# Reordering the turn from the second head pair to the mixture of experts: statistics, drains, norm, filler matmuls, one weight split

## The chip, the cores and the metric

The kernel runs on one core of one Trainium2 chip. The metric is the device time of one launch in microseconds. The time before is 760.16 us, the median of 3 runs (759.25 to 761.29).

## What is computed

One launch runs two transformer layers on 1024 rows of 256 columns, in fp32 accuracy. Each layer is modulated by a vector c: `mod = silu(c) @ wmod` gives shift, scale and gate for its two halves.

- Layer 0: `x += ga * attention(LN(x)*(1+ca)+sa)` (16 heads of 128, 4 key/value heads, rotary, causal), then `x += gb * ffn(LN(x)*(1+cb)+sb)` with a 2:4-sparsified gated unit.
- Layer 1: `x += ga * (h + attention(rmsnorm(h)))` with 4 heads of 64 over 2 key/value heads, not causal, where h is the modulated layer norm; then `x += gb * moe(LN(x)*(1+cb)+sb)`.
- The mixture has one shared expert and 7 routed ones, each `(x1 * silu(x2)) @ w2` with 256 columns in, 2 x 128 inside. A sigmoid of the gate's logits picks two experts per row, and each expert keeps the 146 rows of its highest scores (ties by row order). The kept rows' outputs are weighted by their score and added.

The change touches the end of layer 1's attention and the mixture.

## The kernel before, in words

Each engine has its own program, written out in order; semaphores tie them together. PE is the matmul engine, ACT, DVE and POOL do elementwise work, SP starts transfers. Every fp32 operand of a matmul is kept as a high and a low half, and a product is three matmuls (`product`, L56 to L60): high*high and the two of a high with a low half. Nearly always ACT writes the high half out of PSUM (`..._hi`), and DVE or POOL subtracts it to get the low one (`..._lo`). `keep_warm` (L63) issues filler matmuls into a PSUM area that nobody reads. The kernel is three blocks, with a barrier of all engines between them.

**The end of the attention (`ffn0_attention1`).** The loop over s handles 32 tiles of scores (4 heads x 8 row tiles; HS = 32), with the stages of one tile 3 steps apart (LAG): scores, maximum on DVE, exponential on ACT, scaling on POOL, eight 128x128 transposes on PE (`turn`), high half (`probs_hi`, ACT) and low half (`probs_lo`, DVE). Four tiles make a chunk, whose values product (`attend`, four parts of four matmuls) comes 7 steps behind, so the last chunk (7) is attended in s = 35 to 38, after the last `turn(31)` in s = 34. Its sum is drained by `attended_hi(7)` on ACT and `attended_lo(7)` on DVE. The second head pair's output product is four jobs `out_job(1, j)` of 12 matmuls, each for two row tiles; 0 and 1 need only the chunks of the first row half and run at s = 31 and 32, 2 and 3 need chunk 7 (L1365). DVE adds each to x (`add_out`).
The next layer norm starts here: DVE takes statistics of row tiles 0 to 3 (`final_stats`, at s = 33), aggregates them (`variances`), POOL takes the inverse root (`inverse_roots`), DVE makes a bias of it (`spread`), ACT normalizes four tiles (L1537), PE transposes them (L1361 to L1364), ACT scales and shifts (`ln_h32`), DVE splits the result into `hT` (L1745 to L1749). PE ends the block with 10 fillers (L1367).

**The mixture (`ffn1`).** PE's order: the logits of the first row half (`find_logits(0)`), `up(0)`, `up(1)`, transposes of the second row half (`turn_x`), `up(2)`, `find_logits(1)`, `up(3)`, `turn_logits`, `up(4)`, and then `up(n)` and `count(n - 5)` in turn. `up(n)` is the first product of one expert for one row half, 12 matmuls of 512 columns. The slots are

```
slots = [(0, 0), (1, 0), (2, 0), (0, 1), (1, 1), (2, 1)] + [(e, c) for e in range(3, E8) for c in range(2)]
```

so slot 6 is the first of expert 3. `up(n)` waits for its expert's split weights (`w1_ready`, a count in order of the experts: `split_hi` on ACT, `split_lo` on DVE for 0 and 1, on POOL for the others) and for `mid_done` of slot n - 2, which frees its PSUM banks. Behind each `up`, ACT does `activate`, DVE `middle`, ACT `feed_hi`, POOL `feed_lo`. In the kernel before, POOL splits expert 3 behind `feed_lo(4)`, and ACT's high half of it stands behind `activate(4)`.
The second row half's statistics (tiles 4 to 7) are taken by DVE at the start of this block; its normalized, transposed and scaled rows are split by DVE in `split_x` (L2106), behind `middle(1)`, and `find_logits(1)` waits for that.
Routing: DVE marks the best two (`mark_best`), then ten rounds of `compare` (DVE), `count` (PE) and `raise_cut` (DVE) find each expert's cut; `find_order` (PE) and `weigh` (DVE) settle ties and give `row_weight`. The PSUM areas that `weigh` reads lie in the banks p_y[2] and p_y[3]. Then `down(e)`, the second products, two row tiles at a time (j = 0 to 3, into p_y[j]); the first of them waits for `weight_done`.

Of the kernel before, what the change touches and what calls it, by code (L numbers as in the profile page):

```python
# [16 lines left out]
S = 1024  # L17
# [961 lines left out]
def ffn0_attention1(nc, a, m, sems, sb, split):  # L979
# [6 lines left out]
    with ExitStack() as ctx:  # L986
# [130 lines left out]
        with nc.Block() as block:  # L1117
# [30 lines left out]
            def _(pe):  # L1148
# [195 lines left out]
                for s in range(HS + ATT):  # L1344
                    if s < HS:
                        scores(s)
                    chunk, part = divmod(s - ATT, 4)
                    if s >= ATT and part:
                        attend(chunk, part)
                    if LAG <= s < HS + LAG:  # L1350
                        turn(s - LAG)
                    if s >= ATT and not part:
                        attend(chunk, part)
                    for n, _ in jobs_of(s):
                        if n >= len(first):
                            project(n)
                    for pair_index, j in out_slots.get(s, ()):
                        out_job(pair_index, j)
                pe.wait_ge(turn_lo, 2 * HS)
                pe.wait_ge(ln_normed, len(FIRST_TILES))  # L1360
# [4 lines left out]
                for j in range(2, 4):  # L1365
                    out_job(1, j)
                keep_warm(pe, p_scores[1][:, BANK:S], m.room, 10)  # L1367

            @block.scalar
            def _(act):  # L1370
# [167 lines left out]
                for n in FIRST_TILES:  # L1538
                    act.activation(ln_xn[:, n, :], m.x[:, n, :], ACT.Identity, scale=m.rstd[:, n:n + 1], bias=m.nbias[:, n:n + 1]).then_inc(ln_normed, 1)
                attended_hi(2 * H1 - 1)  # L1540
# [6 lines left out]
            def _(dve):  # L1547
# [175 lines left out]
                for s in range(HS + LAG):  # L1723
# [4 lines left out]
                    if 1 <= s <= HS:  # L1728
                        inverse_sum(s - 1)
                    if s > ATT and (s - ATT) % 4 == 3:  # L1730
                        attended_lo((s - ATT) // 4)
# [7 lines left out]
                    if s == HS + 1:  # L1739
                        final_stats(FIRST_TILES)  # L1740
                        variances(dve, m, chain, FIRST_TILES)
                dve.wait_ge(m.sqrt_out, FFN_ROOTS + CHUNKS + 2)
                spread(dve, m, FIRST_TILES).then_inc(spread_ready, 1)
                attended_lo(2 * H1 - 1)
                for k in range(KD):  # L1745
                    cols = slice(0, BANK)
                    dve.wait_ge(ln_scaled, k + 1)
                    chain.run(dve.tensor_copy(m.hT.hi[:, k, cols], ln_h32[:, k, :]))
                    dve.tensor_tensor(m.hT.lo[:, k, cols], ln_h32[:, k, :], as_f32(m.hT.hi[:, k, cols]), ALU.subtract)  # L1749
                add_out(1, 2)  # L1750
# [98 lines left out]
def ffn1(nc, a, m, sems, sb, split):  # L1849
# [4 lines left out]
    with ExitStack() as ctx:  # L1854
# [63 lines left out]
        with nc.Block() as block:  # L1918
# [15 lines left out]
            def _(pe):  # L1934
# [52 lines left out]
                def down(e):  # L1987
                    pe.wait_ge(w2_ready, e + 1)
                    pe.wait_ge(fed_lo, max(n for n, s in enumerate(slots) if s[0] == e) + 1)
                    if e == 0:  # L1990
                        pe.wait_ge(weight_done, 1)
                    for j in range(PAIRS):
                        if e == 1:
# [33 lines left out]
            def _(act):  # L2027
# [29 lines left out]
                load_table(act, m, ACT.Sigmoid, 2)  # L2057
                activate(0)
                act.wait_ge(spread_ready, 1)
                for n, t in enumerate(LAST_TILES):  # L2060
                    act.activation(xn[:, n, :], m.x[:, t, :], ACT.Identity, scale=m.rstd[:, t:t + 1], bias=m.nbias[:, t:t + 1]).then_inc(normed, 1)  # L2061
                feed_hi(0)
                activate(1)
# [4 lines left out]
                read_logits(0)  # L2068
                feed_hi(1)
                activate(2)  # L2070
                read_logits(1)
                feed_hi(2)
# [7 lines left out]
                for n in range(4, len(slots)):  # L2080
                    e, c = slots[n]
                    activate(n)
                    if c == 1 and 3 <= e + 2 < E8:
# [6 lines left out]
            def _(dve):  # L2090
# [72 lines left out]
                split_lo(1)  # L2163
                for n in LAST_TILES:
                    chain.step(dve.bn_stats(m.stats[:, n, :], m.x[:, n, :]))  # L2165
                variances(dve, m, chain, LAST_TILES)
                dve.memset(aff[:], -1.0).then_inc(aff_cleared, 1)
# [41 lines left out]
            def _(pool):  # L2209
# [19 lines left out]
                pool.wait_ge(m.staged, 48 + 160)  # L2229
                split_lo(2)  # L2230
                inverse_roots(pool, m, LAST_TILES, 11)
                for n in range(len(slots)):
                    e, c = slots[n]
                    feed_lo(n)
                    if c == 1 and 3 <= e + 2 < E8:
# [77 lines left out]
```

## Time and profile before

| | |
|---|---|
| median of 3 runs | 760.16 us |
| profiled execution, own time | 754.2 us |
| its span, first to last instruction | 752.4 us |
| PE busy | 701.7 us (93% of the span), 4301 matmuls |
| DVE / ACT / POOL busy | 551.8 / 441.4 / 386.3 us |
| mean granted PE clock | 0.997 |
| bytes moved | 19.85 MB, mean 26 GB/s |

All is one profiled execution. Times in the rows are us from the start of its span. A busy PE is not a PE at its peak, since matmuls overlap and their ends are modelled: what counts is the time from one start to the next. The number in square brackets behind a row is idle time of that engine just before it, and the instruction that ended it. Granted clock 1.00 is 2.4 GHz.

### The profile page before, as it was taken

The page shows a single profiled execution, that of the slowest core. Times are in us where ns is not written, and L with a number is a line of the kernel's source. Part 1 is how long each engine was busy: PE and PEld are TensorE (multiplying, and loading weights), DVE is VectorE, ACT ScalarE, POOL GpSimd, SP SyncE. Part 2 cuts the span into 40 slices and gives each one's busy share as a digit, 9 for nine tenths or more (in the row PEclk, how much of TensorE's full clock was granted, in tenths as well). Part 3 has the DMA queues.
Part 4 walks back from the last instruction along what each step waited for, and adds up shares of the span by engine and source line. Part 5 has one row for each costly group of instructions (what it writes and reads, how often), then busy time and mean ns, then how long its engine had stood idle before and what let it go on. Part 6 is the DMA issues. An engine that isn't in the chain of part 4 may idle for free. (4 is left out here: it accounts for less than half of the span.)

```text
span 752.4 us, 12234 instructions
## 1 busy us (share of the span) xinstructions
PE 701.7 (93%) x4301; PEld 604.0 (80%) x4301; DVE 551.8 (73%) x1234; ACT 441.4 (59%) x921; POOL 386.3 (51%) x421
## 2 busy tenths in 40 slices
PE   7979989999999999999998889999989999788997
PEld 5858878888888888888887779998767787666787
DVE  4567686768776877677776868989788788564666
ACT  3756656667566666666575545234588777544432
POOL 3876556645864477533662322312498344124773
PEclk9999999999999999999999999999999999999999
DMA  7000001000000000005001023000100000000001
GB/s 258 15 8 8 8 22 57 8 8 15 22 9 15 8 15 8 14 8 182 8 16 42 1 77 94 1 1 5 52 2 1 1 2 1 1 2 1 1 1 58
DMA packets 19131, 19.85 MB, mean 26 GB/s; under 512 B 2174, under 2 KB 17022, under 8 KB 19070
## 3 DMA queue, kind: packets, MB, share of 16 engines
q1 hardware_dynamic: 17950, 18.40, 7.6%
q8 instruction: 35, 0.57, 0.3%
q10 hardware_dynamic: 1120, 0.66, 0.3%
q14 instruction: 26, 0.21, 0.1%
HBM read 18.01 MB, written 1.05 MB: 25 GB/s over the span
## 5 line engine op out<-in xcount | busy, mean ns | idle before, releaser
L909 POOL TENSOR_TENSOR at_swapped<-at_swapped,at_sin 128x512 f32<-128x512 f32 x40 | 52.1, 1303 | 129.3 <-ACT at_swapped L588 129.3
L610 ACT ACTIVATE at_probs<-at_probs,at_negmax 128x128 f32<-128x128 f32 (+7 forms) x128 | 99.6, 778 | 31.8 <-DVE at_negmax L710 29.9
L710 DVE CUSTOM_DVE_ANT_0 at_probs<-at_scores,causal 128x128 f32<-128x128 f32 (+7 forms) x128 | 96.1, 750 | 17.4 <-PE at_scores L60 16.3
L501 PE MATMUL at_turn<-ident_sb,at_probs 128*128 128x128 f32 x576 | 85.0, 274 | 11.2 <-DVE at_full_T_lo L726 9.1
L501 PEld LDWEIGHTS at_turn<-ident_sb,at_probs 128*128 128x128 f32 x576 | 66.5, 140 | 19.8 <-issue 11.4
L603 ACT ACTIVATE at_edge_T_hi<-at_turn 128x128 fp32r<-128x128 f32 (+3 forms) x128 | 55.5, 434 | 33.4 <-PE at_turn L501 33.0
L58 PE MATMUL at_scores<-at_kT_hi,room 128*128 128x512 f32 (+1 forms) x192 | 66.3, 345 | 3.4 <-DVE at_negmax L710 3.4
L603 ACT ACTIVATE at_full_T_hi<-at_turn 128x512 fp32r<-128x512 f32 x64 | 38.2, 597 | 49.8 <-PE at_turn L501 47.6
L59 PE MATMUL at_scores<-at_kT_lo,room 128*128 128x512 f32 (+1 forms) x192 | 66.6, 347 | 0.0
L60 PE MATMUL at_scores<-at_kT_hi,room 128*128 128x512 f32 (+1 forms) x192 | 66.4, 346 | 0.0
L726 DVE TENSOR_TENSOR at_edge_T_lo<-at_turn,at_edge_T_hi 128x128 fp32r<-128x128 f32 (+3 forms) x128 | 61.3, 479 | 1.3 <-ACT at_edge_T_hi L603 0.8
L913 POOL TENSOR_TENSOR at_plain<-at_plain,at_swapped 128x512 f32<-128x512 f32 x40 | 51.8, 1296 | 6.1 <-POOL at_swapped L909 0.5
L740 DVE SCALAR_TENSOR_TENSOR x<-at_proj,at_rinv,x 128x256 f32<-128x256 f32 x122 | 52.8, 474 | 0.1
L731 DVE TENSOR_TENSOR at_att_lo<-at_att,at_att_hi 128x512 fp32r<-128x512 f32 x32 | 22.1, 692 | 38.4 <-ACT at_att_hi L617 38.4
L726 DVE TENSOR_TENSOR at_full_T_lo<-at_turn,at_full_T_hi 128x512 fp32r<-128x512 f32 x64 | 44.1, 689 | 7.1 <-ACT at_full_T_hi L603 5.4
L58 PEld LDWEIGHTS at_scores<-at_kT_hi,room 128*128 128x128 f32 x192 | 36.2, 188 | 9.5 <-issue 2.6
L918 POOL TENSOR_TENSOR room<-at_plain,room 128x512 fp32r<-128x512 f32 x32 | 41.4, 1292 | 2.7
L700 DVE TENSOR_TENSOR at_plain<-at_scores,at_cos 128x512 f32<-128x512 f32 x30 | 20.8, 692 | 29.9 <-ACT at_swapped L588 29.9
L58 PE MATMUL at_att<-at_edge_T_hi,at_v 128*128 128x512 f32 (+3 forms) x128 | 42.0, 328 | 0.0
L60 PE MATMUL at_att<-at_edge_T_hi,at_v 128*128 128x512 f32 (+3 forms) x128 | 41.3, 323 | 0.0
L58 PE MATMUL at_proj<-at_wo_hi,at_att_hi 128*128 128x256 f32 x122 | 39.5, 324 | 1.9 <-DVE x L740 1.8
L59 PE MATMUL at_att<-at_edge_T_lo,at_v 128*128 128x512 f32 (+3 forms) x128 | 41.1, 321 | 0.0
(446 smaller groups left out, 2257.7 us busy)
## 6 DMA issues: line engine op xcount, KB each, us to landing
at_wq_in<-L_attn_Wqkv SPq DMA_DIRECT2D x16, 128.0 KB, 2.2
at_wo_in<-L_attn_Wo SPq DMA_DIRECT2D x16, 128.0 KB, 2.0
staging<-L_ffn_routed_w SPq DMA_DIRECT2D x7, 256.0 KB, 4.3
wmod<-L_wmod SPq DMA_DIRECT2D x2, 768.0 KB, 4.3
at_wmod<-L_wmod SPq DMA_DIRECT2D x1, 1024.0 KB, 9.3
staging<-L_ffn_w_gate SPq DMA_DIRECT2D x1, 1024.0 KB, 5.3
staging<-L_ffn_w_up SPq DMA_DIRECT2D x1, 1024.0 KB, 7.4
staging<-L_ffn_w_down SPq DMA_DIRECT2D x1, 1024.0 KB, 9.8
```

The lines of the kernel that those rows point to most:

```text
L58: pe.matmul(out, left.hi, right.hi, start=start, stop=False)
L59: pe.matmul(out, left.hi, right.lo, start=False, stop=False)
L60: return pe.matmul(out, left.lo, right.hi, start=False, stop=stop)
L501: mm = pe.transpose(p_turn[t % 2][:, b - b0, :], probs[:, s % 4, b * P:(b + 1) * P], m.ident[:, :])
L603: act.activation(turned_columns(c, b0, b1, i % 4).hi, p_turn[t % 2][:, 0:b1 - b0, :], ACT.Copy)\
L610: act.activation(row, row, ACT.Exp, scale=-1.0, bias=negmax[:, unit % 4:unit % 4 + 1], accum_out=rowsum[:, unit // NT % 2, i:i + 1])\
L710: dve.tensor_tensor_reduce(out=probs[:, s % 4, 0:width], in0=p_scores[s % 2][:, 0:width], in1=m.causal[:, S - width:], scale=-1.0, scalar= ...
L726: dve.tensor_tensor(out.lo, p_turn[t % 2][:, 0:b1 - b0, :], as_f32(out.hi), ALU.subtract).then_inc(turn_lo, 1)
L740: ins = dve.scalar_tensor_tensor(out=rows, in0=bank[:, t * DM:(t + 1) * DM], scalar=rinv[:, head % 2, 2 * j + t:2 * j + t + 1], in1=rows, ...
L909: turning = pool.tensor_tensor(swapped[:, r % 2, :], swapped[:, r % 2, :], sin[:, cols], ALU.mult)
L913: chain.step(pool.tensor_tensor(turned, turned, swapped[:, r % 2, :], ALU.add))
L918: pool.tensor_tensor(out.lo[:, cols], turned, as_f32(out.hi[:, cols]), ALU.subtract).then_inc(rope_done, 1)
```

## The change

It moves the statistics of the first row half to two places (tiles 0 and 1 at s = 33, tiles 2 and 3 with the aggregation at s = 34, behind `attended_lo(6)` and `probs_lo(31)`), takes the drain of chunk 7 between the second and third normalized tile on ACT, puts `out_job(1, 2)` ahead of the norm's transposes and `add_out(1, 2)` ahead of the splits on DVE, takes the statistics of tiles 4 and 5 already in this block, and has 5, 6 and 8 fillers in three places in the place of 10 at the end. In the mixture, DVE takes statistics of tiles 6 and 7 alone and ahead of expert 1's low half, POOL takes the roots ahead of expert 2's low half, ACT changes the order of `activate(1)`, `feed_hi(0)` and `read_logits(0)` and drops one `load_table`, expert 3 is split behind `read_logits(1)` (ACT) and `feed_lo(2)` (POOL), and `down(0)` waits for `weight_done` at j = 2.

```diff
--- before.py
+++ after.py
@@ -1356,15 +1356,18 @@
                             project(n)
                     for pair_index, j in out_slots.get(s, ()):
                         out_job(pair_index, j)
+                    if s == HS + LAG - 1:
+                        keep_warm(pe, p_scores[1][:, BANK:S], m.room, 5)
                 pe.wait_ge(turn_lo, 2 * HS)
+                keep_warm(pe, p_scores[1][:, BANK:S], m.room, 6)
+                out_job(1, 2)
                 pe.wait_ge(ln_normed, len(FIRST_TILES))
                 for k in range(KD):
                     for n in FIRST_TILES:
                         mm = pe.transpose(turn_banks[k][:, n * P:(n + 1) * P], ln_xn[:, n, k * P:(k + 1) * P], m.ident[:, :])
                     mm.then_inc(ln_turned, 1)
-                for j in range(2, 4):
-                    out_job(1, j)
-                keep_warm(pe, p_scores[1][:, BANK:S], m.room, 10)
+                out_job(1, 3)
+                keep_warm(pe, p_scores[1][:, BANK:S], m.room, 8)
 
             @block.scalar
             def _(act):
@@ -1536,8 +1539,9 @@
                             job_high(n)
                 act.wait_ge(spread_ready, 1)
                 for n in FIRST_TILES:
+                    if n == 2:
+                        attended_hi(2 * H1 - 1)
                     act.activation(ln_xn[:, n, :], m.x[:, n, :], ACT.Identity, scale=m.rstd[:, n:n + 1], bias=m.nbias[:, n:n + 1]).then_inc(ln_normed, 1)
-                attended_hi(2 * H1 - 1)
                 for k in range(KD):
                     act.wait_ge(ln_turned, k + 1)
                     act.activation(ln_h32[:, k, :], turn_banks[k], ACT.Identity, scale=m.modcol[:, 1, 8 + k:9 + k], bias=m.modcol[:, 1, 6 + k:7 + k])\
@@ -1727,6 +1731,8 @@
                         job_low(len(first) - 1)
                     if 1 <= s <= HS:
                         inverse_sum(s - 1)
+                    if s == HS + 1:
+                        final_stats(range(0, 2))
                     if s > ATT and (s - ATT) % 4 == 3:
                         attended_lo((s - ATT) // 4)
                     if s >= LAG:
@@ -1736,18 +1742,19 @@
                             job_low(n)
                     for pair_index, j in out_slots.get(s, ()):
                         add_out(pair_index, j)
-                    if s == HS + 1:
-                        final_stats(FIRST_TILES)
+                    if s == HS + 2:
+                        final_stats(range(2, 4))
                         variances(dve, m, chain, FIRST_TILES)
                 dve.wait_ge(m.sqrt_out, FFN_ROOTS + CHUNKS + 2)
                 spread(dve, m, FIRST_TILES).then_inc(spread_ready, 1)
                 attended_lo(2 * H1 - 1)
+                add_out(1, 2)
+                final_stats(range(4, 6))
                 for k in range(KD):
                     cols = slice(0, BANK)
                     dve.wait_ge(ln_scaled, k + 1)
                     chain.run(dve.tensor_copy(m.hT.hi[:, k, cols], ln_h32[:, k, :]))
                     dve.tensor_tensor(m.hT.lo[:, k, cols], ln_h32[:, k, :], as_f32(m.hT.hi[:, k, cols]), ALU.subtract)
-                add_out(1, 2)
                 add_out(1, 3)
 
             @block.gpsimd
@@ -1987,9 +1994,9 @@
                 def down(e):
                     pe.wait_ge(w2_ready, e + 1)
                     pe.wait_ge(fed_lo, max(n for n, s in enumerate(slots) if s[0] == e) + 1)
-                    if e == 0:
-                        pe.wait_ge(weight_done, 1)
                     for j in range(PAIRS):
+                        if e == 0 and j == 2:
+                            pe.wait_ge(weight_done, 1)
                         if e == 1:
                             pe.wait_ge(shared_added, j + 1)
                         elif e:
@@ -2054,21 +2061,21 @@
                 split_hi(0)
                 split_hi(1)
                 split_hi(2)
-                load_table(act, m, ACT.Sigmoid, 2)
+                read_logits(0)
                 activate(0)
                 act.wait_ge(spread_ready, 1)
                 for n, t in enumerate(LAST_TILES):
                     act.activation(xn[:, n, :], m.x[:, t, :], ACT.Identity, scale=m.rstd[:, t:t + 1], bias=m.nbias[:, t:t + 1]).then_inc(normed, 1)
+                activate(1)
                 feed_hi(0)
-                activate(1)
                 for k in range(KD):
                     act.wait_ge(turned, k + 1)
                     act.activation(h32[:, k, :], p_turn[k], ACT.Identity, scale=m.modcol[:, 1, 8 + k:9 + k], bias=m.modcol[:, 1, 6 + k:7 + k])\
                         .then_inc(scaled_h, 1)
-                read_logits(0)
                 feed_hi(1)
                 activate(2)
                 read_logits(1)
+                split_hi(3)
                 feed_hi(2)
                 activate(3)
                 act.wait_ge(aff_cleared, 1)
@@ -2080,7 +2087,7 @@
                 for n in range(4, len(slots)):
                     e, c = slots[n]
                     activate(n)
-                    if c == 1 and 3 <= e + 2 < E8:
+                    if c == 1 and 4 <= e + 2 < E8:
                         split_hi(e + 2)
                     feed_hi(n)
                 for e in range(1, E8):
@@ -2160,10 +2167,10 @@
                     dve.tensor_tensor(row_weight[:, :, :], score[:, :, :], kept[:, :, :], ALU.mult).then_inc(weight_done, 1)
 
                 split_lo(0)
-                split_lo(1)
-                for n in LAST_TILES:
+                for n in range(6, 8):
                     chain.step(dve.bn_stats(m.stats[:, n, :], m.x[:, n, :]))
                 variances(dve, m, chain, LAST_TILES)
+                split_lo(1)
                 dve.memset(aff[:], -1.0).then_inc(aff_cleared, 1)
                 chain.step(dve.memset(best2[:], -1.0))
                 dve.memset(ones[:], 1.0)
@@ -2227,12 +2234,14 @@
 
                 chain = m.pool_chain.on(pool)
                 pool.wait_ge(m.staged, 48 + 160)
+                inverse_roots(pool, m, LAST_TILES, 11)
                 split_lo(2)
-                inverse_roots(pool, m, LAST_TILES, 11)
                 for n in range(len(slots)):
                     e, c = slots[n]
                     feed_lo(n)
-                    if c == 1 and 3 <= e + 2 < E8:
+                    if n == 2:
+                        split_lo(3)
+                    elif c == 1 and 4 <= e + 2 < E8:
                         split_lo(e + 2)
                     elif n >= 6:
                         split_w2(n // 2 - 3 if n < 13 else n - 9)
```

## Rows read from the trace of the kernel before

**Rows 1.** PE's timeline, end of attention: start, length, line, tile, idle before.

```profile
647.10 1.16 PE L1277 MATMUL l_turn<-ident_sb,staging 128*128 128x128 f32 x8
651.32 0.50 PE L1291 MATMUL l_att_sum<-l_pT_hi,l_v 128*128 128x512 f32 x1 [3.06 <-DVE l_pT_lo L1651]
...
655.14 1.04 PE L1363 MATMUL l_turn<-ident_sb,l_probs 128*128 128x128 f32 x8
656.92 0.36 PE L58 MATMUL l_scores<-l_wo_hi,l_att_hi 128*128 128x256 f32 x1 [0.74 <-DVE l_att_lo L1656]
...
659.86 2.44 PE L67 MATMUL l_scores<-room 128*128 128x512 f32 x10
662.60 0.39 PE L58 MATMUL ff_y<-hT_hi,gate_w_hi 128*7 128x512 f32 x1 [0.30 <-PEq L1117]
```

**Rows 2.** Who waited for whom, 640 to 726 us: total us, times, longest us.

```profile
PE ff_y L58 <- DVE hT_lo L2111: 1.6, 1, 1.6
...
PE ff_y L58 <- DVE ff_row_weight L2160: 0.9, 1, 0.9
```

**Rows 3.** PE's timeline in the mixture, around up(6).

```profile
686.04 0.41 PE L1972 MATMUL ff_y<-ff_above,ff_ones 128*128 128x64 bf16 x8
689.75 0.50 PE L58 MATMUL ff_px<-hT_hi,room 128*128 128x512 f32 x1 [3.31 <-POOL ff_w_lo L2214]
...
694.43 0.48 PE L58 MATMUL ff_px<-hT_hi,room 128*128 128x512 f32 x1
...
697.56 0.48 PE L58 MATMUL ff_px<-hT_hi,room 128*128 128x512 f32 x1
```

**Rows 4.** The chain that ended last, same stretch: start, length, engine, tile.

```profile
685.78 0.69 DVE ff_mid L2104
...
687.20 1.27 POOL ff_fed_lo L2220
688.47 1.24 POOL ff_w_lo L2214
```

**Rows 5.** The windows view: stretch, length, engines' busy time, granted clock.

```profile
648.00:652.00 4.00, 0.94 (x6) 0.61 (x5) 3.27 (x12) 1.52 (x4) 1.04 (x1) 1.00 0.00 0
690.00:694.00 4.00, 4.00 (x12) 3.06 (x11) 0.00 (x0) 0.00 (x0) 2.19 (x2) 0.57 0.00 0
```

**Rows 6.** DVE's timeline at the end of the attention.

```profile
646.26 1.29 DVE L1651 TENSOR_TENSOR l_pT_lo<-l_turn,l_pT_hi 128x512 fp32r<-128x512 f32 x2 [1.29 <-ACT l_pT_hi L1464]
647.47 1.40 DVE L1668 BATCH_NORM_STATS2 stats<-x 128x6 f32<-128x256 f32 x4
...
649.31 0.17 DVE L191 TENSOR_SCALAR vareps<-meanvar 128x4 f32<-128x4 f32 x1
...
649.99 1.28 DVE L1651 TENSOR_TENSOR l_pT_lo<-l_turn,l_pT_hi 128x512 fp32r<-128x512 f32 x2
...
655.97 0.69 DVE L1656 TENSOR_TENSOR l_att_lo<-l_att_sum,l_att_hi 128x512 fp32r<-128x512 f32 x1 [4.64 <-ACT l_att_hi L1482]
656.64 0.43 DVE L1748 CAST hT_hi<-staging 128x512 fp32r<-128x512 f32 x1
...
658.77 0.68 DVE L1662 TENSOR_TENSOR x<-l_scores,x 128x512 f32<-128x512 f32 x1
```

**Rows 7.** ACT's timeline at the end of the attention.

```profile
647.77 1.13 ACT L1464 ACTIVATE l_pT_hi<-l_turn 128x512 fp32r<-128x512 f32 x2 [0.18 <-PE l_turn L1277]
651.37 2.08 ACT L1539 ACTIVATE l_probs<-x,nbias,rstd 128x256 f32<-128x256 f32 x4 [2.48 <-DVE nbias L204]
655.34 0.60 ACT L1482 ACTIVATE l_att_hi<-l_att_sum 128x512 fp32r<-128x512 f32 x1 [1.89 <-PE l_att_sum L1292]
```

**Rows 8.** The timeline of POOL: the inverse root, feed_lo(1).

```profile
649.56 1.04 POOL L198 TENSOR_TENSOR rstd<-vareps,power 128x4 f32<-128x4 f32 x1 [6.54 <-DVE vareps L191]
...
673.37 1.48 POOL L2220 TENSOR_TENSOR ff_fed_lo<-ff_mid,ff_fed_hi 128x512 fp32r<-128x512 f32 x1 [1.60 <-ACT ff_fed_hi L2044]
```

**Rows 9.** The timeline of DVE in split_x, the second low half.

```profile
673.77 1.63 DVE L2111 TENSOR_TENSOR hT_lo<-staging,hT_hi 128x512 fp32r<-128x512 f32 x1
```

## The prediction

> **What bounds the kernel now.** I read the page first: PE is busy 93% of the span, and its granted clock stands at 9 tenths or more in all 40 slices, so only places where PE waits or runs slowly are worth anything. The chain that ended last runs through the mixture, and nearly all of it there is PE's own matmuls, so I went through PE's timeline from the end of the attention to the last product and wrote down each wait and what ended it. Five places stand out. (a) PE stands 3.06 us before the last chunk's values product [rows 1]. (b) The attention's block ends with 2.44 us of fillers, and the mixture begins 0.30 us behind them [rows 1]. (c) PE waits 1.6 us for the second low half of split_x [rows 2]. (d) PE waits 3.31 us before up(6), for POOL's low half of expert 3 [rows 3, 4]. (e) PE waits 0.9 us before the first down, for the row weights [rows 2]. Behind (d) there is a second loss: the windows view shows a granted clock of 0.57 from 690 to 694 us, so mostly the lower level, 1.2 GHz [rows 5]. From up(6) to up(7), with one count, PE needs 694.43 - 689.75 = 4.68 us; the next such step takes 697.56 - 694.43 = 3.13 us [rows 3].
>
> All times below are those of the profiled execution (754.2 us in all, 752.4 us of it span); where a place has moved I still use the old clock times. The runs shown have a median of 760.16 us, 5.96 us more; I take the difference that I work out and subtract it from either.
>
> **(a, b) The end of the attention.** Statistics of four tiles take 1.40 us, so 0.70 us for two [rows 6]. Before, DVE takes them and the aggregation from 647.47 to 649.48, ahead of the low halves of turn(31), which are done at 649.99 + 1.28 = 651.27; PE starts the last chunk 0.05 us later [rows 1, 6]. Now tiles 0 and 1 come ahead of 646.26, where DVE waited anyway, and the others behind turn(31). ACT has both high halves done at 647.77 + 1.13 = 648.90 [rows 7], the last low half takes half of 1.28 us, so it is done near 649.6 and the chunk starts at 649.65: 1.67 us sooner. The 5 fillers, at 2.44 / 10 = 0.24 us each, take 1.2 us behind turn(31) (647.10 + 1.16 = 648.26) and end by 649.5, inside the wait.
> The rest follows by distances of before. The chunk's matmuls take 655.14 - 651.32 = 3.82 us, and ACT's drain starts 655.34 - 651.32 = 4.02 us behind their start [rows 1, 7], at 653.67. By then two tiles must be normalized: the aggregation ends 1.3 us behind 649.6, the root takes 1.04 us [rows 8], so ACT starts near 652.3 and has two at 2.08 / 4 = 0.52 us [rows 7] done at 653.35, just in time. DVE's drain comes 655.97 - 655.34 = 0.63 us later, at 654.30, and out_job(1, 2) 656.92 - 655.97 = 0.95 us behind that [rows 1, 6, 7], at 655.25. Six fillers from 653.47 end at 654.9, inside that wait. An output job takes (659.86 - 656.92) / 2 = 1.47 us; the eight transposes about 0.9 us between them [rows 1]. So PE has out_job(1, 2) done at 656.7, the transposes at 657.6, out_job(1, 3) at 659.1, and 8 fillers of 1.95 us at 661.05. DVE starts behind out_job(1, 2), near 656.95: one add 0.68, two statistics 0.70, four splits 658.77 - 656.64 = 2.13, one add 0.68 [rows 6], in sum 4.19 us, to 661.15. Both engines end together, 1.15 us ahead of 659.86 + 2.44 = 662.30. I take -1.1. Bounds: -1.67 (all of the sooner start) and 0 (a late normalization holds ACT's drain, which is now queued behind two tiles, and the adds and splits behind it on DVE).
>
> **(c) The start of the mixture up to find_logits(1).** That the second half's normalized rows are ready sooner brings nothing: ACT takes them behind activate(0), which waits for up(0) either way. Two statistics fewer (0.70 us) are worth nothing for the same reason. Expert 1's low half is queued behind the aggregation, but up(1) starts a whole up (3.13 us less a count) behind up(0); I price it at 0, at most one root, 1.04 us [rows 8], if POOL's and DVE's operations hold each other up. The dropped load_table is a small operation in a wait of ACT, 0. What changes is split_x. activate(1) no longer stands behind feed_hi(0), so middle(1) and split_x start about 0.4 us sooner (an estimate: an ACT drain of a 128x512 tile takes 0.60 us [rows 7], less some overlap with its neighbours). But read_logits(0) has gone from between, so feed_hi(1), and POOL's feed_lo(1) behind it, start sooner too, into the middle of split_x. The rows show what that costs: the second low half took 1.63 us, where a DVE operation on two inputs of this shape takes 0.68 [rows 6, 9], while POOL's feed_lo(1) ran from 673.37 for 1.48 us, more than the 1.27 of another one [rows 4, 8]. So before, one meeting cost 0.95 us. With one such meeting of a full POOL operation now: -0.4 + 1.27 - 0.95 = -0.08. With feed_lo(0)'s end in the way of the first split as well (about 0.45 us, an estimate from its place): +0.4. I take +0.2, between them. Bounds: no meeting at all, -0.4 - 0.95 = -1.35; two whole POOL operations, -0.4 + 2.54 - 0.95 = +1.2.
> The Trainium skill ("SBUF — State Buffer", section "Who interferes with whom") says that DVE and POOL share a pair of ports, that the one that issues first holds it for its whole instruction, and that the other blocks entirely, for DVE instructions with two inputs in SBUF and for copies in their two-port mode. The rows agree: 673.37 + 1.48 = 674.85 lies inside the 1.63 us, and the rest is about one undisturbed low half. This rule speaks against the edit: by it the sum of (c) is near the +0.2 to +0.4 above, without it it would be -1.35.
>
> **(d) Expert 3.** Now ACT makes the high half behind read_logits(1) and POOL the low half behind feed_lo(2), while PE has up(3) to up(5) to do, some 9 us; POOL needs 1.24 us for it [rows 4]. What is late next is mid_done of slot 4: middle(4) ends at 685.78 + 0.69 = 686.47 [rows 4], so up(6) starts near 686.55 in the place of 689.75: -3.2. On ACT the moved high half (0.60 us, the shape of [rows 7]) stands ahead of feed_hi(2) and activate(3), and PE gets to the end of up(3) only some 2 us later; on POOL, feed_lo(3) is queued behind the moved low half and has its whole slot for it. No transfer is moved by any edit. The clock: PE then stands no longer than about 1.8 us in (c) (1.6 + 0.2) and 0.1 us here. The 3.06 us of (a) left the granted clock at 1.00 in the windows view from 648 to 652, the 3.31 us of (d) were followed by 0.57 [rows 1, 3, 5]. So I take up(6) at full speed: 4.68 - 3.13 = -1.55. Bounds: 0 and -1.55.
>
> **(e) down(0).** j = 0 and 1 write banks that weigh does not read. They are 12 matmuls, as many as an output job, 1.47 us; the wait was 0.9 us [rows 2], so weight_done is there before j = 2: -0.95. Bounds: -0.95 and 0, the latter if DVE, which adds the shared output in order behind weigh, is late for down(1); its adds of 0.68 us [rows 6] keep up with jobs of half 1.47.
>
> **Sum.** -1.1 + 0.2 - 3.2 - 1.55 - 0.95 = -6.6 us. For the profiled execution 754.2 - 6.6 = 747.6; for the median 760.16 - 6.6 = **753.6 us**. The bounds of all parts together, up(1)'s 1.04 among them, are -8.7 and -1.0: 751.4 and 759.2.
>
> **Rivals.**
> *Split_x meets no POOL operation:* 1.55 us more gain, 752.0. For it: feed_lo(0) and feed_lo(1) could fall on either side. Against: the meeting that rows 8 and 9 show, and both are nearer now.
> *The clock falls elsewhere:* the 1.8 us of (c) come after a stretch with several short waits, and the loss of 1.55 us moves there: 755.1. For it: the 3.31 us were followed by the lower level and the 3.06 us were not [rows 1, 3, 5], so little tells the two apart. Against: 1.8 us is well short of both.
> *POOL becomes the bound:* it loses 4.7 us of lead on the slots behind. Two slots take PE 6.26 us; two low halves and one weight split come to 2 x 1.27 + 1.24 [rows 4], and the two operations of a second weight's split, half as wide, to about 1.5 (an estimate), 5.3 in sum. If meetings with DVE stretch these past PE by 0.35 us a slot, nine slots cost 3.2: 756.8.
> *The split isn't what up(6) waited for:* the wait is put down to POOL, and another semaphore would come within the same time. Then (d) brings nothing and the gain is 1.1 - 0.2 + 0.95 = 1.85: 758.3. Against: the chain of waits has the low half end at 689.71 and PE start at 689.75 [rows 3, 4].
> *Slower:* the lower clock level sets in during the wait of (c) and stays until count(0). From 675.7 to 686.0 PE has 10.3 us of matmuls at full speed; at 1.2 GHz they take up to twice as long: 753.6 + 10.3 = 763.9. It decides from 6.6 us on, two thirds of that stretch. Against: the one low stretch [rows 3, 5] cost 1.55 us and was over within one up.
>
> **How the numbers follow.** The forecast has 0.62, no meeting 0.10, the clock 0.12, POOL 0.06, the split for nothing 0.06, slower 0.04. Within 0.3% (2.3 us, what a measurement here can tell from no change) is 757.9 to 762.4. Faster holds the first four, less a little for the bounds of the forecast, which reach 759.2: 0.88; same 0.08; slower 0.04. The range is 751.0 to 757.2: it takes in the no-meeting, the clock and the POOL case.
>
> **What would show it.** PE's timeline: the last chunk starts about 1.4 us behind turn(31)'s end in the place of 3.06; fillers fill both waits; the block's last DVE and PE operations end within 0.2 us of each other; the wait before find_logits(1) is about 1.8 us; up(6) follows count(0) with 0.1 us between; the granted clock stays at 1.00 in that stretch; down(0) follows find_order at once. The prediction is wrong if up(6) still waits a microsecond or more, if the clock falls below 0.9 anywhere between 640 and 690 us, or if up and count together take more than 3.2 us in slots 7 to 15.

## The result, and the profile after

The changed kernel takes 747.96 us (median of 4 runs, 747.14 to 749.88) where the kernel before took 759.89 (4 runs, 759.25 to 761.29, three of them those of the time before): a ratio of 0.9844 [0.9821, 0.9868], or -11.9 us. The direction was right. The time lies below the predicted range (751.0 to 757.2), and the gain is nearly twice the -6.6 us of the sum.

The trace of after does not show such a gain. Its profiled execution took 749.88 us, 4.3 us less than that of before and 2.3 us more than the 747.6 forecast for it; its span is 748.1 us. The last turn(31) starts at 649.39 us in after and at 647.10 in before [rows 1], though the code up to there is the same; from it to the end of the span it is 98.7 us, in before 105.3 (98.67 and 105.31 with the ends of the spans, 748.06 and 752.41 us, to the hundredth). The difference is -6.6 us, which is the sum of the prediction. The question of this study is therefore why 6.6 us of work saved made the median 9 to 12 us shorter.

The stretch first, place by place. This is PE's timeline of after at the end of the attention (start, length, line, operation, tile, idle before); it answers to [rows 1].

```profile
649.39 1.16 PE L1277 MATMUL l_turn<-ident_sb,staging 128*128 128x128 f32 x8
650.31 1.40 PE L67 MATMUL l_scores<-room 128*128 128x512 f32 x5
652.03 0.50 PE L1291 MATMUL l_att_sum<-l_pT_hi,l_v 128*128 128x512 f32 x1 [0.32 <-DVE l_pT_lo L1655]
...
655.84 1.55 PE L67 MATMUL l_scores<-room 128*128 128x512 f32 x6
657.62 0.36 PE L58 MATMUL l_scores<-l_wo_hi,l_att_hi 128*128 128x256 f32 x1 [0.23 <-DVE l_att_lo L1660]
...
661.41 1.99 PE L67 MATMUL l_scores<-room 128*128 128x512 f32 x8
663.83 0.40 PE L58 MATMUL ff_y<-hT_hi,gate_w_hi 128*7 128x512 f32 x1 [0.43 <-PEq L1117]
```

The last chunk starts 2.64 us behind the start of turn(31), before 4.22: -1.58 us, where the prediction had -1.67. The 3.06 us wait is fillers now, with 0.32 us left. Set back by the 2.29 us that this execution is late, out_job(1, 2) was forecast for 657.54 and starts at 657.62. DVE's and ACT's timelines show the new order that makes it so; they answer to [rows 6, 7].

```profile
650.68 1.29 DVE L1655 TENSOR_TENSOR l_pT_lo<-l_turn,l_pT_hi 128x512 fp32r<-128x512 f32 x2
651.89 0.74 DVE L1672 BATCH_NORM_STATS2 stats<-x 128x6 f32<-128x256 f32 x2
...
659.31 0.69 DVE L1666 TENSOR_TENSOR x<-l_scores,x 128x512 f32<-128x512 f32 x1 [1.95 <-PE l_scores L60]
660.04 0.75 DVE L1672 BATCH_NORM_STATS2 stats<-x 128x6 f32<-128x256 f32 x2
...
662.82 0.68 DVE L1666 TENSOR_TENSOR x<-l_scores,x 128x512 f32<-128x512 f32 x1
```

```profile
654.61 1.10 ACT L1544 ACTIVATE l_probs<-x,nbias,rstd 128x256 f32<-128x256 f32 x2 [3.42 <-DVE nbias L204]
656.04 0.60 ACT L1485 ACTIVATE l_att_hi<-l_att_sum 128x512 fp32r<-128x512 f32 x1 [0.33 <-PE l_att_sum L1292]
```

The low halves run ahead of the statistics of tiles 2 and 3, and ACT's drain comes between the two pairs of normalized tiles. DVE's last add ends at 663.50 and PE's last filler at 663.40, 0.1 us apart, as forecast; because out_job(1, 2) and its add now lie inside, the block from there to find_logits(0) takes 6.21 us, before 5.68. Together (a) and (b) bring -1.06 us (forecast -1.1).

In the mixture, PE's timeline of after around find_logits(1), up(6) and down(0), which answers to [rows 2, 3]:

```profile
676.90 0.40 PE L58 MATMUL ff_y<-hT_hi,gate_w_hi 128*7 128x512 f32 x1 [1.64 <-DVE hT_lo L2118]
...
687.48 0.41 PE L1979 MATMUL ff_y<-ff_above,ff_ones 128*128 128x64 bf16 x8
688.04 0.47 PE L58 MATMUL ff_px<-hT_hi,room 128*128 128x512 f32 x1 [0.16 <-DVE ff_mid L2111]
...
691.15 0.48 PE L58 MATMUL ff_px<-hT_hi,room 128*128 128x512 f32 x1
...
694.27 0.48 PE L58 MATMUL ff_px<-hT_hi,room 128*128 128x512 f32 x1
...
719.31 0.32 PE L1991 MATMUL ff_y<-ff_equal,ff_ones 128*128 128x56 bf16 x7
719.49 0.36 PE L58 MATMUL ff_y<-ff_w_hi,ff_fed_hi 128*128 128x256 f32 x1
```

up(6) follows its count at once: 0.56 us in the place of 3.71, -3.15 (forecast -3.2), and what it waits for now is middle(4), as the prediction named it. From up(6) to up(7) it is 3.11 us in the place of 4.68, -1.57 (forecast -1.55). down(0) stands directly behind find_order: -1.08 us (forecast -0.95), with +0.02 from there to the end. In before its first matmul waited for the row weights (PE's timeline of before):

```profile
722.60 0.32 PE L1984 MATMUL ff_y<-ff_equal,ff_ones 128*128 128x56 bf16 x7
723.86 0.36 PE L58 MATMUL ff_y<-ff_w_hi,ff_fed_hi 128*128 128x256 f32 x1 [0.94 <-DVE ff_row_weight L2160]
```

The slots 8 to 15, up to find_order, take 24.77 us in both traces, so POOL did not become the bound. The windows of after, which answer to the second of [rows 5], show PE at the full granted clock (1.00, 2.4 GHz) where before it was 0.57 (the granted clock is the number ahead of the last two):

```profile
688.00:692.00 4.00, 3.96 (x24) 3.14 (x25) 2.53 (x8) 2.80 (x5) 2.51 (x2) 1.00 0.00 0
690.00:694.00 4.00, 4.00 (x25) 2.94 (x23) 2.08 (x6) 1.71 (x3) 2.57 (x2) 1.00 0.00 0
```

Place (c) comes to +0.21 us (forecast +0.2), but not by one mechanism. The timelines of DVE and POOL in after, which answer to [rows 8, 9]:

```profile
667.94 1.26 DVE L204 SCALAR_TENSOR_TENSOR nbias<-meanvar,rstd 128x4 f32<-128x4 f32 x1 [0.47 <-POOL rstd L198]
...
673.17 0.81 DVE L2117 CAST hT_hi<-staging 128x512 fp32r<-128x512 f32 x1
674.01 0.69 DVE L2118 TENSOR_TENSOR hT_lo<-staging,hT_hi 128x512 fp32r<-128x512 f32 x1
674.62 1.50 DVE L2117 CAST hT_hi<-staging 128x512 fp32r<-128x512 f32 x1
```

```profile
667.88 1.31 POOL L2221 TENSOR_TENSOR ff_w_lo<-staging,room 128x512 fp32r<-128x512 f32 x1
672.40 1.29 POOL L2227 TENSOR_TENSOR ff_fed_lo<-ff_mid,ff_fed_hi 128x512 fp32r<-128x512 f32 x1 [3.21 <-ACT ff_fed_hi L2051]
674.25 1.58 POOL L2227 TENSOR_TENSOR ff_fed_lo<-ff_mid,ff_fed_hi 128x512 fp32r<-128x512 f32 x1 [0.56 <-ACT ff_fed_hi L2051]
```

Both feed_lo meet a cast of split_x, as I had it: the casts take 0.81 and 1.50 us, where two others of this shape take 0.41 and 0.42. What I had not seen is the third meeting. POOL now makes split_lo(2) behind the inverse root, so it starts 0.06 us ahead of the bias of the norm, and that operation on 128x4 numbers takes 1.26 us; at the end of the attention the same line took 0.16. A fourth meeting goes the other way round: POOL's inverse root starts 0.25 us behind DVE's low half of expert 1 and takes 1.31 us, where it took 1.01 in before.

### The profile page after: what moved, and what is told of

It is laid out like the page before. It is cut to its first block and busy times, and to the rows that moved or that the text cites. A ratio compares the mean times of both kernels' runs of the same rounds, so it can differ in the third digit from the quotient of the medians.

```text
span 748.1 us, 12251 instructions
## 1 busy us (share of the span) xinstructions
PE 704.1 (94%) x4310; PEld 606.5 (81%) x4310; DVE 553.2 (74%) x1234; ACT 442.1 (59%) x920; POOL 387.3 (52%) x421
## 5 line engine op out<-in xcount | busy, mean ns | idle before, releaser
L198 POOL TENSOR_TENSOR rstd<-vareps,power 128x4 f32<-128x4 f32 (+2 forms) x11 | 11.0, 997 | 66.7 <-DVE vareps L191 66.7
```

## The experiments

Every comparison is with runs of the kernel before beside it on the same chip, and a difference in us is worked out from the ratio. Theory A (the one wait): the clock is lost only behind the 3.31 us wait, the numbers of the profiled execution hold, and the rest is chance. Theory B (the clock): the profiled execution of before was a lucky one, the typical one loses the clock in more places, and the change removes such a loss too.

**The kernel before once more**, unchanged.

> The unchanged kernel again, to see where its usual execution loses the 5.9 us by which its median (759.9) stands above the profiled one (754.2). Theory 'clock at the waits': its executions have a lower mean clock than 0.997 (below 0.99), and a trace shows the clock low behind the 3.06 us wait of the last chunk or for longer behind the 3.31 us wait of up(6). Rival 'start': the extra time lies in the first 120 us. Rival 'profile only': clock and span are as in the first profile and the extra lies outside of the span. Time against the kernel before: 0 +- 1 us in all.

758.69 us (12 runs) against 757.18 (32 runs), 1.0025 [1.0003, 1.0047]: +1.9 us between two sets of the same code, clear of its own interval, so a single difference of 2 us below says little by itself. What it gave is the list of runs: of the 84 executions of this kernel here and in the comparisons below, two (752.73 and 753.95) are no longer than the 754.2 us on which the prediction rests. Their mean granted clock lies between 0.982 and 0.997, in the profiled one at 0.997. In each of the four sets of 32, 12, 17 and 11 runs, time goes with the clock time lost, (1 - clock) x time: the correlation is 0.93, 0.93, 0.90 and 0.97, and a us of lost clock time comes with 0.62, 0.49, 0.52 and 0.55 us of time. The windows of this second execution show where it is lost:

```profile
10.00:20.00 10.00, 7.35 (x32) 6.12 (x33) 7.40 (x22) 4.21 (x7) 5.36 (x7) 0.83 0.65 238
40.00:50.00 10.00, 6.88 (x29) 5.26 (x30) 5.00 (x11) 5.62 (x14) 9.29 (x10) 0.84 0.00 2
50.00:60.00 10.00, 8.80 (x49) 7.70 (x47) 8.89 (x21) 6.97 (x15) 3.93 (x6) 0.82 0.05 13
...
690.00:700.00 10.00, 8.89 (x45) 6.85 (x46) 2.79 (x9) 2.97 (x5) 4.65 (x4) 0.83 0.00 0
```

The granted clock is 0.82 to 0.84 in three windows before 60 us, where the first profile had 1.00; the fourth line is the loss behind up(6), which the first profile has too. This execution is 1.4 us longer than the first, and all of that lies ahead of turn(31), which starts at 648.53 us; from there on it takes the same 105.3 us. So for this one execution the rival 'start' holds, and no loss behind the 3.06 us wait is seen. In the traces of the other kernels, whose code up to 640 us is the same, the clock falls in some of these windows, or at 550 us, and in others not, and turn(31) starts anywhere from 646.21 to 650.29 us, which the falls alone do not explain (the earliest start is in a trace with two of them, the first profile has none and starts at 647.10). These losses lie ahead of all that the change touches.

**Expert 3 alone.**

```
                 read_logits(1)
+                split_hi(3)
...
-                    if c == 1 and 3 <= e + 2 < E8:
+                    if n == 2:
+                        split_lo(3)
+                    elif c == 1 and 4 <= e + 2 < E8:
```

> The kernel before with expert 3 split sooner, nothing else. By the forecast's terms: -3.2 for the wait, -1.55 for the clock, about -4.75 us. Theory 'clock at the waits', if the extra sits behind up(6): -6 to -10. If the extra sits at the attention's end or at the start: -4.75.

752.79 us (9 runs), 0.9942 [0.9920, 0.9964]: -4.4 us, where part (d) had -4.75. The steps to up(6) and to up(7) are 3.13 and 1.55 us shorter. But its trace shows what the profile of before did not, behind the unchanged 3.06 us wait (PE's timeline, then the windows):

```profile
654.51 0.79 PE L1291 MATMUL l_att_sum<-l_pT_hi,l_v 128*128 128x512 f32 x1 [3.06 <-DVE l_pT_lo L1651]
655.10 0.63 PE L1292 MATMUL l_att_sum<-l_pT_lo,l_v 128*128 128x512 f32 x1
...
657.53 0.39 PE L1292 MATMUL l_att_sum<-l_pT_lo,l_v 128*128 128x512 f32 x1
```

```profile
654.00:658.00 4.00, 3.49 (x10) 2.78 (x11) 0.52 (x2) 2.07 (x4) 0.00 (x0) 0.58 0.00 0
```

The matmuls of the last chunk take 0.63 us in the place of 0.39 at a granted clock of 0.58, and the stretch from the last chunk to out_job(1, 2) is 6.87 us in the place of 5.60. The sentence of the prediction that the 3.06 us wait leaves the clock alone holds in some executions and not in this one. The -6 to -10 us that the theory had for an extra loss behind up(6) did not come.

**The end of the attention alone**: the change's edits of the attention, and tiles 6 and 7 alone in the mixture's statistics.

```
+                    if s == HS + LAG - 1:
+                        keep_warm(pe, p_scores[1][:, BANK:S], m.room, 5)
...
+                keep_warm(pe, p_scores[1][:, BANK:S], m.room, 6)
+                out_job(1, 2)
...
+                out_job(1, 3)
+                keep_warm(pe, p_scores[1][:, BANK:S], m.room, 8)
```

> The change's edits to the end of the attention alone (order of statistics, drains, output jobs, fillers; the mixture's statistics are of tiles 6 and 7 only), the rest as before. By the forecast's terms: -1.1 us. Theory 'clock at the waits', if the extra sits behind the 3.06 us wait: -2.5 to -6. Rivals 'start' and 'profile only': -1.1.

754.18 us (12 runs), 0.9957 [0.9936, 0.9977]: -3.3 us [-4.8, -1.7], where the prediction had -1.1. In its trace the end of the attention is 1.09 us shorter, and find_logits(0) to turn_x another 0.24 (7.10 us, before 7.34): the two statistics fewer, which the prediction priced at 0, were worth that. The 3.31 us wait of up(6) is there in this trace, and the clock did not fall behind it (PE's timeline, then the windows):

```profile
689.61 0.50 PE L58 MATMUL ff_px<-hT_hi,room 128*128 128x512 f32 x1 [3.31 <-POOL ff_w_lo L2221]
```

```profile
690.00:694.00 4.00, 4.00 (x25) 3.10 (x24) 0.93 (x4) 0.60 (x1) 2.06 (x2) 1.00 0.00 0
```

So a wait of that length is followed by the lower level in some executions and not in others. Of the traces in which nothing fills the 3.06 us, two have the fall (expert 3 alone and the next experiment), two have not (the kernel before, twice); of those with the 3.31 us unfilled, three have it (the kernel before twice, and the last chunk's fillers below) and this one has not.

**Fillers in the waits of the kernel before.** These take no wait away; they give PE something to do in it, so what they bring is the clock alone. First 13 before up(6):

```
+                    if n == FIRST_ROUND + 1:
+                        keep_warm(pe, p_y[0][:, :, :].rearrange("p a b -> p (a b)"), m.room, 13)
```

> The kernel before with 13 filler matmuls of 512 columns (0.24 us each, 3.1 us) between count(0) and up(6), so that PE is busy while it waits for expert 3; the wait itself stays. By the forecast's terms: -1.55 us (the clock's part). Theory 'clock at the waits', if the extra sits behind up(6): -4 to -7. If it sits elsewhere: -1.55.

756.13 us (12 runs) against 757.18, 0.9977 [0.9957, 0.9997]: -1.7 us [-3.3, -0.2], about the 1.55 of the prediction, and not the theory's -4 to -7. Then 12 more ahead of the last chunk:

```
+                    if s == HS + LAG - 1:
+                        keep_warm(pe, p_scores[1][:, BANK:S], m.room, 12)
```

> The kernel before with 12 fillers before the last chunk's values product and 13 before up(6); all waits stay. Theory 'clock at the waits': the clock no longer falls at either place, in its trace the granted clock is 1.00 from 640 to 750 us, and the gain is about 3 us, some 1.5 more than with the fillers before up(6) alone. Rival 'the extra lies elsewhere' (start of the kernel, outside of the span): -1.8 as with those alone, or less.

754.63 us (7 runs) against 758.72, 0.9944 [0.9923, 0.9964]: -4.2 us [-5.8, -2.7]. In its trace the fillers take up both waits, and the granted clock stays at 1.00 (PE's timeline, then the windows):

```profile
650.22 3.02 PE L67 MATMUL l_scores<-room 128*128 128x512 f32 x12
653.52 0.50 PE L1291 MATMUL l_att_sum<-l_pT_hi,l_v 128*128 128x512 f32 x1 [0.29 <-DVE l_pT_lo L1653]
...
688.42 3.23 PE L67 MATMUL ff_y<-room 128*128 128x512 f32 x13
691.97 0.50 PE L58 MATMUL ff_px<-hT_hi,room 128*128 128x512 f32 x1 [0.32 <-POOL ff_w_lo L2218]
```

```profile
640.00:750.00 110.00, 103.38 (x662) 84.92 (x660) 71.69 (x193) 47.96 (x90) 51.67 (x56) 1.00 0.02 5
```

And those 12 alone:

> The kernel before with 12 fillers before the last chunk's values product alone; both waits stay. With fillers at both places the gain was 4.2 us (interval 2.7 to 5.8), at up(6) alone 1.8 (0.2 to 3.3). Theory 'the clock is lost behind both waits in most executions': -2 to -2.8 us. Rival 'in half of them at most', as two of four traces show: -0.8.

755.55 us (12 runs) against 758.13, 0.9967 [0.9951, 0.9983]: -2.5 us [-3.7, -1.3]. The two alone add up to the two together, 1.7 + 2.5 = 4.2, more closely than their intervals warrant. The prediction had 1.55 of this and nothing for the last chunk. With the fillers the waits last as before: from the start of turn(31) to the last chunk it is 4.22 us with and without them, from count(0) to up(6) 3.79 us with them and 3.71 without. So this is not a shorter wait.

The mean clocks of the single executions say the same, and they point at losses that no trace caught. Of the 84 executions of the kernel before, 41 have a mean clock below 0.988; of the 90 of all kernels in which one or both of the two waits are filled or shortened, none has. With the last chunk's fillers alone the mean of the lost clock time falls from 9.7 to 6.1 us, by 3.6, while one loss in a trace is (1 - 0.58) x 4 = 1.7 us. Of the 41 none was traced, so where they lose the rest is not shown.

**The changed kernel again, twice.**

> The changed kernel unchanged, beside the kernel before on the chip of this call, with more executions of each. Theory 'clock at the waits': the gain is the 5.1 us of waits and reordering that the traces show, plus 0.6 us for each us of clock lost that goes away; with the kernel before at a lost clock of 8 to 10 us and the changed one at 3.5 to 5 that is 2 to 3.5 us: -7.5 to -9, and the changed kernel's executions spread less. Rival 'the first comparison holds': -11.9. Rival 'the profiled difference holds': -6.6.

> The changed kernel once more, beside the kernel before on this call's chip. Theory 'waits 5.0 us, clock 4.2 us': -9.2 us, give or take 1.5. Rival 'the first comparison holds': -11.9. Rival 'the profiled difference holds': -6.6.

750.07 us (6 runs) against 758.72 on one chip, 0.9881 [0.9856, 0.9905], and 748.87 (6 runs) against 758.13, 0.9885 [0.9861, 0.9908]: -9.0 and -8.7 us. Their stretches from turn(31) on are 98.71 and 98.70 us. The -11.9 us of the first comparison, 4 runs against 4, was not seen again. The changed kernel loses 4.6 and 6.0 us of clock time less than the kernel before beside it; at the 0.49 and 0.52 us of time that each us came with, that is 2.2 and 3.1 us.

**The changed kernel without the 5 and 6 fillers**, once and once more; the other edits stay.

```
-                    if s == HS + LAG - 1:
-                        keep_warm(pe, p_scores[1][:, BANK:S], m.room, 5)
...
-                keep_warm(pe, p_scores[1][:, BANK:S], m.room, 6)
```

> The changed kernel without the 5 and the 6 fillers in its two waits (the 8 at the block's end stay). The waits are then 1.5 and 1.7 us of idle PE. Theory 'clock at the waits': such waits are short of the 3.1 us that lost the clock in some executions, so the clock falls in few of them: 0 to +1 us against the changed kernel, and mean clock 0.990 to 0.994. Rival 'the fillers do the work': the clock falls behind one of the two in most executions: +1.5 to +3 us.

> The changed kernel without the 5 and the 6 fillers once more. The first trace of it lost the clock behind the wait of out_job(1, 2) (7.15 us for a stretch of 5.59), but its times were those of the changed kernel. Theory 'waits of 1.5 us lose the clock in some executions': the stretch is 5.6 or 7.1 us in this trace, the gain against the kernel before is -7.5 to -9. Rival 'the clock falls there in every execution': -7 to -7.7 and 7.1 us. Rival 'the fillers do nothing': -8.7 to -9.3 and 5.6 us.

749.79 us, 0.9881 [0.9855, 0.9907], and 750.17, 0.9884 [0.9861, 0.9908] (6 runs each): no difference from the changed kernel that these runs can tell. The first trace, though, loses the clock behind a wait of 1.48 us, half of the 3.06 us (PE's timeline, then the windows):

```profile
651.87 0.74 PE L1291 MATMUL l_att_sum<-l_pT_hi,l_v 128*128 128x512 f32 x1 [1.48 <-DVE l_pT_lo L1652]
652.41 0.63 PE L1292 MATMUL l_att_sum<-l_pT_lo,l_v 128*128 128x512 f32 x1
```

```profile
652.00:656.00 4.00, 4.00 (x11) 3.14 (x12) 1.19 (x8) 1.09 (x2) 1.04 (x1) 0.58 0.00 0
```

It costs 1.56 us there (7.15 us to out_job(1, 2) in the place of 5.59); in the second trace the clock stays at 1.00 and it is 5.58. So the fillers may guard against a loss that comes in some executions, but their worth is not shown: the times don't tell them from nothing.

**No meetings in (c)**: POOL's split_lo(2) waits for the bias, and its feeds for the end of split_x.

```
                 inverse_roots(pool, m, LAST_TILES, 11)
+                pool.wait_ge(spread_ready, 1)
                 split_lo(2)
+                pool.wait_ge(hT_ready, KD)
                 for n in range(len(slots)):
```

> The changed kernel, and POOL waits before two operations: before expert 2's low half until DVE has made the bias of the second norm, before feed_lo(0) until split_x is done. So POOL reads nothing in SBUF while DVE makes the bias or runs split_x. Theory 'POOL and DVE block each other there': the bias takes 0.16 us in the place of 1.26 and turn_x starts 0.2 to 0.4 us sooner, split_x takes 2.1 us in the place of 3.7 and the wait before find_logits(1) falls from 1.64 to below 0.3: the stretch from the last turn to the end is 96.7 to 97.1 us in the place of 98.7, and the time is 1.5 to 2 us below the changed kernel's. Rival 'split_x is late for another reason' or 'what waits for feed_lo(0) is late next': no change, or up to 1 us slower.

> The changed kernel with POOL's two waits once more, for a second interval. Theory 'POOL and DVE block each other there': again 1.5 to 2 us below the changed kernel, so -10.5 to -11.5 us against the kernel before, clock 0.994 or more in the median, stretch from the last turn to the end near 97.1 us. Rival 'the first comparison with it was luck': -8.7 to -9.3, as the changed kernel.

746.79 us (4 runs) against 758.13 and 748.26 (6 runs) against 759.67: 0.9856 [0.9831, 0.9881] and 0.9856 [0.9833, 0.9878], -10.9 us both times. It is 2.1 us below the changed kernel and 1.9 us below that without fillers, each run beside it (748.87 and 750.17); with 4 and 6 runs whose ranges overlap, the 1.5 us of the trace below is the surer figure. DVE in its trace, and PE's wait behind it:

```profile
666.59 0.16 DVE L204 SCALAR_TENSOR_TENSOR nbias<-meanvar,rstd 128x4 f32<-128x4 f32 x1 [0.46 <-POOL rstd L198]
...
671.74 0.41 DVE L2117 CAST hT_hi<-staging 128x512 fp32r<-128x512 f32 x1
672.18 0.69 DVE L2118 TENSOR_TENSOR hT_lo<-staging,hT_hi 128x512 fp32r<-128x512 f32 x1
672.80 0.42 DVE L2117 CAST hT_hi<-staging 128x512 fp32r<-128x512 f32 x1
```

```profile
674.00 0.39 PE L58 MATMUL ff_y<-hT_hi,gate_w_hi 128*7 128x512 f32 x1 [0.52 <-DVE hT_lo L2118]
```

The stretch from turn(31) on is 97.13 us, 1.54 less than in after: 0.43 up to turn_x, where the bias lies, and 1.12 from there to find_logits(1), where split_x lies. These are the starts of turn_x on PE, before, after and without the meetings:

```profile
669.94 1.09 PE L1944 MATMUL ff_y<-ident_sb,staging 128*128 128x128 f32 x8
671.37 1.09 PE L1951 MATMUL ff_y<-ident_sb,staging 128*128 128x128 f32 x8 [0.30 <-ACT staging L2068]
669.59 1.09 PE L1951 MATMUL ff_y<-ident_sb,staging 128*128 128x128 f32 x8
```

POOL's first feed comes 3.0 us later, counted from turn(31), and PE waits for POOL nowhere behind it: the slots 8 to 15 again take 24.77 us. The Trainium skill ("SBUF — State Buffer", section "Who interferes with whom") has whichever of DVE and POOL issues second block entirely while the other holds the ports they share. These traces agree: in after, POOL starts first in the three meetings, and each of the three DVE operations ends 0.01 to 0.3 us behind POOL's, even the one that takes 0.16 us by itself.

## Why the prediction was right in the trace and wrong in the time

**(a, b)**, **(d)** and **(e)** came within 0.15 us each, and the sum of the stretch within 0.05 us. Part of that closeness is luck: (c) came to its +0.2 by other terms than mine. Without the three meetings it is -1.34 us against before, next to my lower bound of -1.35, but 0.23 of it lie ahead of turn_x (7.34 - 7.11), where I had priced the two statistics fewer at 0, and 1.11 behind it (5.52 - 4.41). The meetings with both feeds cost 1.12 us, where I had 1.27 and a part of 0.45, and the bias cost 0.43, which I had not listed. The rival without a meeting was priced at 1.55 us, and the kernel without meetings gained 1.54 in its trace. The rivals of the POOL bound and of the split for nothing fell, and so did the slower one and that of the clock falling in (c): the clock stays at 1.00 after the wait of 1.64 us there.

**The step that failed** is the clock term, and with it the way from the profile to the median. The prediction says that the 3.06 us of (a) left the clock at 1.00, takes one loss of 1.55 us, and gives -1.55 and 0 as its bounds. Filling the two waits measured -4.2 us [-5.8, -2.7]: the term was mis-sized by about 2.7 us, and by the single fillings (-2.5 and -1.7) it was so at the place that I had excluded from one trace. Taking it in: the stretch without the clock is 105.31 - 1.55 - 98.67 = 5.1 us shorter, and with 4.2 for the clock that is 9.3; the three comparisons of the changed kernel gave -9.0, -8.7 and -11.9, and those without its fillers -9.0 and -8.8. Of the first, the -11.9, some 2.6 us are left over.

The sign that I passed over was in the numbers in front of me. The profiled execution lay 5.96 us below the median, its clock stood at 0.997, and I carried those 5.96 us along as a constant. By the correlations above such a difference goes with lost clock time, and the part of it that is lost at PE's waits can be given back by a change to them. Not all of it is: the 1.4 us of the second trace of before lie ahead of everything that the change touches. Theory A falls by the fillers: at an unchanged length of every wait they make the kernel faster, and by more than the one loss that the profile showed. Theory B stands as far as the two waits go; that the 41 executions of the lowest clocks lose it there is inferred from the fillers and the mean clocks, not seen in a trace.

**What stays open.** A trace with the loss at the last chunk is 1.3 to 1.6 us longer there, and only some executions have it, so the traces account for less than the 2.5 us [1.3, 3.7] that its fillers brought; the lower end of that interval is what fits. By the traces the clock could give at most 1.55 + 1.53 us (the second from the trace with fillers before up(6), 7.13 - 5.60), in sum -8.2 us, inside the intervals of the two larger comparisons ([-10.9, -7.2] and [-10.5, -7.0]) but not of the first ([-13.6, -10.0]). In the first the kernel before took 759.25 us or more, which 55 of the 84 executions stay below, and the changed kernel 747.96 where it later took 750.07 and 748.87. Whether the losses before 60 us fell unevenly on these 4 and 4 runs was not tried. Nor is it settled what decides, in one execution, whether the clock falls behind a given wait.

## What to carry to other kernels

Before a difference worked out in one trace is taken off a median, compare that execution's own time and clock with the other runs: where they lie apart, what separates them may be a cost that the change moves too. A wait of PE has two prices, its length and, in some executions, a stretch at the lower clock behind it, and one trace shows only one outcome of the second. Where DVE is on the path, look at what POOL starts in the same microsecond: here two waits of POOL, which cost nothing on PE, brought 1.5 us.

## What the chip showed that I had not expected

The lower clock came behind a wait of 1.48 us in one trace and not behind 3.31 us in another. At the last chunk the matmuls took 0.63 us in the place of 0.39 for some 3 us in each of the three traces that show it, which cost 1.3 to 1.6 us. And a DVE operation of 0.16 us took 1.26 beside one of POOL.
